# Causal mask by a GpSimd select on the exponentiated scores instead of mask matmuls, and both sets of dispatch writes in one block

## The chip, the cores and the metric

The program runs on one core of one Trainium2 chip. The metric is the device time of one execution in microseconds (us). A core has a matmul engine (TensorE, PE in the profile), a vector engine (VectorE, DVE), an activation engine (ScalarE, ACT), a general engine (GpSimd, POOL) and a queue that starts transfers (SyncE, SP). Each runs its own list of instructions in order and waits for the others on semaphores.

## The reference, cut to what matters

Two transformer-like layers on x (4, 1024, 128). Layer 0 is a state-space scan and a mixture of 16 experts. Layer 1 is attention with 16 heads of 8 with a bias by distance, then a block with causal attention and a top-2 mixture of 16 experts with capacity. The change touches two places of this last block:

```
scores = jnp.einsum('bhqd,bhkd->bhqk', q, k)
causal = jnp.tril(jnp.ones((s, s), bool))          # s = 1024 here
scores = jnp.where(causal, scores, neg)
attn = jax.nn.softmax(scores, axis=-1)
ctx = jnp.einsum('bhqk,bhkd->bhqd', attn, v)
hidden = resid + (ctx @ o_w + o_b)
...
xt = layer_norm(hidden, ln2_w, ln2_b).reshape(T, D)
...
xin = jnp.einsum('tec,td->ecd', dispatch, xt)      # each token to its two experts' slots
...
moe_out = jnp.einsum('tec,ecd->td', combine, eout)
return resid + moe_out
x = x + gb * that
```

## The kernel before

**Attention.** `attend` serves both attention layers; `a.causal` tells them apart. It works in 16 units, one for each batch b and group g of four heads. A unit has two passes that run in different units at the same time:

- Row maxima of a later unit: `top_turn` multiplies queries by keys for 128 queries and up to 512 keys, for two heads at once (L1095), and VectorE takes the maximum over the keys (L1199). When all turns of a unit are read, the maxima are transposed (L1088), negated (L1196) and moved by four transfers from SyncE (L1033) into the last row of the query operand, so that the second pass subtracts them inside its matmul.
- Scores, exponentials and values of this unit: `score_pair` multiplies keys by queries (L1123), so that the scores lie with 128 keys on the partitions and up to 512 queries along the row. ScalarE exponentiates them (L1236) from one of three PSUM banks into a ring of 16 slots in SBUF. `value_turn` multiplies the values by the exponentials and adds up in bank 7 (L1144).

A piece is one key tile i and one half of the queries; in the causal case queries before i * 128 are left out. The causal list has 12 pieces n: (i=0..3, first half), then (i=0..3, second half, all 512 wide), then (i=4..7, second half). Pieces 0 to 3 and 8 to 11 begin on the diagonal and are 512, 384, 256 and 128 wide; pieces 4 to 7 don't touch it. Each piece has four heads, so two calls of `score_pair` and four exponentials.

TensorE's order is written out in `run`: for each piece n and each pair of heads one `score_pair`, then the top turns that `plan_tops` puts there, then half of the value turn of piece n - LAG (LAG = 2; the last two pieces of a unit are valued in the first two pieces of the next). So the value turn of piece n comes behind the first score turn of piece n + 2. A score turn waits until the exponentials of the banks that it needs are done; a value turn waits for the four exponentials of its piece; exponentials wait for the value turn of four pieces ago, which frees their ring slots.

The causal mask is made on TensorE. `add_mask` adds four small bf16 matmuls behind a score or a top matmul on the diagonal: identity times a triangle of -1e30, in two halves of 64 rows, for two heads (L1105). GpSimd has one job in the causal stage, the copy of the next unit's values (L1250, `next_values`). In the biased layer it also multiplies exponentials by the bias near the diagonal (L1275, in `bias`), and there the value turn waits for it as well, on the semaphore `scaled`.

**Routing and experts.** `route` computes the two experts and slots of each token. GpSimd then writes the tokens into the experts' rows in DRAM, 32 indirect transfers for each of the two choices (`send_copies`, L1669). The first 32 are issued at the end of `route`. The block then ends, which is a barrier over all engines, and `experts` begins with the second 32, while VectorE multiplies the residual stream by its gate and adds it to x (L1850, L1852). SyncE waits there for all 64 and reads the first two experts' rows back (L1727).

**Constants.** One transfer loads all constants (`cst`), the mask parts among them; VectorE converts them to bf16 (`half`, L159).

Of the kernel before, what the change touches and what calls it, by code (L numbers as in the profile page):

```python
# [20 lines left out]
P = 128  # L21
# [3 lines left out]
TB = L // P  # L25
# [24 lines left out]
C_HALF = C_FLIP + P  # L50
C_W = C_HALF + 6 * P

# [801 lines left out]
def attend(nc, k, a):  # L854
# [44 lines left out]
    def near(n):  # L899

        i, half, q0, q1 = PIECES[n]
        lo, hi = max(q0, (i - 1) * P), min(q1, (i + 2) * P)
        return (lo, hi) if lo < hi and not causal else None
# [50 lines left out]

    NEARS = [n for n in range(NP_) if near(n)]

    with ExitStack() as c:
# [17 lines left out]
        stored = sem("stored")  # L975
        few_in, few_out, inverted = (sem(n) for n in ("few_in", "few_out", "inverted"))
        (a_filled, a_read, joined, b_filled, exped, scaled, pv_done, o_copied,
# [46 lines left out]
        with nc.Block() as block:  # L1024
# [48 lines left out]
            def _(pe):  # L1073
                first.tensor(pe)

                def top_turn(b, g, n):


                    turn = unit(b, g) * NA_ + n
                    slot = A_BANK + 2 * ((g * NA_ + n) % 2)  # L1080
                    if n == 0:
                        pe.wait_ge(loads[g], (b + 1) * NLOAD)

                    if not (isinstance(turn, int) and turn < 2):
                        pe.wait_ge(a_read, turn - 1)
                    if n == NT_:
                        pe.wait_ge(joined, unit(b, g) + 1)
                        nc.tensor.transpose(k.ps[0:HG * TB, slot, 0:P], top[:, 0, :, :].rearrange("p j i -> p (j i)"),  # L1088
                                            k.cst[:, C_ID:C_ID + P]).then_inc(a_filled, 1)
                        return  # L1090
                    pair, i, k0, k1 = TURNS[n]
                    diag = causal and k0 <= i * P < k1
                    for x in range(2):
                        rows = slice(64 * x, 64 * x + ROWS)
                        ins = nc.tensor.matmul(k.ps[:, slot + x, 0:k1 - k0], qop[rows, g, pair, i * P:(i + 1) * P],  # L1095
                                               kop[rows, g, pair, k0:k1], start=True, stop=not diag)
                    if diag:
                        ins = add_mask(slot, i * P - k0, 1)
                    ins.then_inc(a_filled, 1)

                def add_mask(bank, at, which):
                    for part in range(2):
                        for x in range(2):
                            rows = slice(64 * x, 64 * x + 64)
                            ins = nc.tensor.matmul(k.ps[:, bank[x] if isinstance(bank, tuple) else bank + x, at:at + P],  # L1105
                                                   k.half[rows, part, 0, :], k.half[rows, part, which, :],
                                                   start=False, stop=part == 1)
                    return ins

                def score_pair(b, g, n, pair):  # L1110
# [8 lines left out]
                    bank = (B_BANK + bank_of(g, t), B_BANK + bank_of(g, t + 1))  # L1119
                    diag = causal and q0 == i * P  # L1120
                    for x in range(2):
                        rows = slice(64 * x, 64 * x + ROWS + 1)
                        ins = nc.tensor.matmul(k.ps[:, bank[x], 0:q1 - q0], kop[rows, g, pair, i * P:(i + 1) * P],  # L1123
                                               qop[rows, g, pair, q0:q1], start=True, stop=not diag)
                    if diag:
                        ins = add_mask(bank, 0, 2)
                    ins.then_inc(b_filled, 1)
# [115 lines left out]
            def _(pool):  # L1243
# [20 lines left out]
                def bias(b, g):  # L1264

                    u = unit(b, g)
                    for n in NEARS:
                        i, half, q0, q1 = PIECES[n]
                        if n == NEARS[len(NEARS) // 2]:
                            next_values(b, g)  # L1270
                        lo, hi = near(n)
                        for j in range(HG):
# [7 lines left out]
                values(0, 0)  # L1280
                units(pool, next_values if causal else bias)

# [205 lines left out]
def route(nc, k, m, r):  # L1488
# [6 lines left out]
    with ExitStack() as c:  # L1495
        def sb(name, shape, dt=F32):
# [19 lines left out]
            ("logits", "e_ready", "chain", "ch_ready", "counts", "turned", "moved"))  # L1516
        ex_go, to_ready, ids_set = (nc.alloc_semaphore("ro_" + n) for n in ("ex_go", "to_ready", "ids_set"))

# [9 lines left out]
        with nc.Block() as block:  # L1528
# [32 lines left out]
            def _(act):  # L1561
# [16 lines left out]
                for b in range(B):  # L1578
                    ts = slice(b * TB, (b + 1) * TB)
                    nc.scalar.copy(r.xt[:, 1, ts, 0:D], r.xt[:, 0, ts, 0:D])  # L1580

            @block.gpsimd
            def _(pool):
# [6 lines left out]
                pool.wait_ge(act_plain, NT // 2)  # L1590
                send_copies(nc, k, r, 0)

            @block.vector
            def _(dve):
# [67 lines left out]
                L_(vec.tensor_scalar(col2[:], col2[:], KEEP, None, ALU.mult))  # L1662
                vec.tensor_tensor(r.g[:], r.g[:], col2[:].unsqueeze(1).broadcast_to([P, 2, NT]), ALU.mult)


# [15 lines left out]
def experts(nc, k, m, r):  # L1681
# [3 lines left out]
    with ExitStack() as c:  # L1685
        def sb(name, shape, dt=F32):
# [16 lines left out]
        got = [nc.alloc_semaphore(f"ex_got{s}") for s in range(4)]  # L1703
        first, both, gated, summed, x_plain, ids_kept, x_stored = (
            nc.alloc_semaphore("ex_" + n) for n in ("first", "both", "gated", "summed", "x_plain", "ids_kept", "x_stored"))
        chain = nc.alloc_semaphore("ex_chain")

        with nc.Block() as block:  # L1708
            @block.gpsimd
            def _(pool):  # L1710
                send_copies(nc, k, r, 1)
                for e in range(E):
# [132 lines left out]
            def _(dve):  # L1845

                for b in range(B):
                    h = r.hidden[:, b * TB:(b + 1) * TB, :]
                    xs = k.x[:, b * TB:(b + 1) * TB, :]
                    nc.vector.tensor_tensor(h, h, k.row[:, 2, b:b + 1, :].broadcast_to([P, TB, D]), ALU.mult).then_inc(chain, 1)  # L1850
                    dve.wait_ge(chain, b + 1)
                    nc.vector.tensor_tensor(xs, xs, h, ALU.add).then_inc(x_plain, 1)  # L1852
                dve.wait_ge(consts_in, 32)
# [24 lines left out]
                def add(n):  # L1878

                    xs = k.x[:, 4 * n:4 * n + 4, :]  # L1880
                    dve.wait_ge(gated, n + 1)
                    dve.wait_ge(x_plain, B)
                    nc.vector.tensor_tensor(xs, xs, back[:, 1, n % 4, :, :], ALU.add).then_inc(summed, 1)  # L1883
# [22 lines left out]
def causal_sublayer(nc, k, m):  # L1906
# [5 lines left out]
    with ExitStack() as c:  # L1912
# [28 lines left out]
        r.to = sb("to", [P, 2, NT], I32)  # L1941
        r.sent = nc.alloc_semaphore("cs_sent")
        r.g = sb("g", [P, 2, NT])
# [25 lines left out]
def program(nc, m):  # L1969
    with ExitStack() as c:  # L1970
# [15 lines left out]
        k.kop = sb("kop", [P, NG, 2, L], BF16)  # L1986
        k.half = sb("half", [P, 2, 3, P], BF16)

# [22 lines left out]
def constants():  # L2011
# [9 lines left out]
    a[:, C_MB:C_MB + P] = np.where(i[None, :] < i[:, None], NEG, 0.0)  # L2021
    half = a[:, C_HALF:C_W].reshape(P, 2, 3, P)
    for part in range(2):
        for base in range(2):
            rows = slice(64 * part, 64 * part + 64)
            for x, at in enumerate((C_ID, C_MA, C_MB)):
                half[64 * base:64 * base + 64, part, x] = a[rows, at:at + P]
# [81 lines left out]
```

## Time and profile before

| | us |
|---|---|
| median of 3 runs | 2185.87 (2176.83 to 2188.6) |
| the profiled execution's own time | 2184.34 |
| its span in the profile | 2182.5 |
| PE matmul busy over the span | 1741.0 |
| DVE busy | 1553.3 |
| ACT busy | 1188.9 |
| POOL busy | 765.8 |

Busy times are sums over stages with different limits. The causal attention stage lies from about 1355 to 1848 us of the span, the biased one ends near 1290, routing lies between 1884 and 2013, the experts after it. A row of the timeline gives start, duration of the merged instructions, engine, line, output and inputs, how many were merged, and in square brackets the idle time before them and who ended it. Rows of TensorE may overlap, since matmuls are pipelined; PEld is its weight load.

### The profile page before, as it was taken

The page shows a single profiled execution, that of the slowest core. Times are in us where ns is not written, and L with a number is a line of the kernel's source. Part 1 is how long each engine was busy: PE and PEld are TensorE (multiplying, and loading weights), DVE is VectorE, ACT ScalarE, POOL GpSimd, SP SyncE. Part 2 cuts the span into 40 slices and gives each one's busy share as a digit, 9 for nine tenths or more (in the row PEclk, how much of TensorE's full clock was granted, in tenths as well). Part 3 has the DMA queues.
Part 4 walks back from the last instruction along what each step waited for, and adds up shares of the span by engine and source line. Part 5 has one row for each costly group of instructions (what it writes and reads, how often), then busy time and mean ns, then how long its engine had stood idle before and what let it go on. Part 6 is the DMA issues. An engine that isn't in the chain of part 4 may idle for free. (4 is left out here: it accounts for less than half of the span.)

```text
span 2182.5 us, 45999 instructions
## 1 busy us (share of the span) xinstructions
PE 1741.0 (80%) x15779; PEld 799.5 (37%) x15780; DVE 1553.3 (71%) x2677; ACT 1188.9 (54%) x2290; POOL 765.8 (35%) x938
## 2 busy tenths in 40 slices
PE   5799999986899989989999545988998997500992
PEld 2666666652122222222222222333333332500671
DVE  4778887879899889989996288776776772551223
ACT  3232222242688878878888442776776776300432
POOL 1100000023577777767777432000000000156454
PEclk8799999997799999999999866999999999555996
DMA  2193000004010011001000305011111110411444
GB/s 78 59 136 78 0 0 0 0 21 129 16 36 19 19 24 31 19 20 36 19 19 14 88 22 144 19 37 24 32 37 37 36 23 15 125 35 52 128 133 135
DMA packets 93751, 103.52 MB, mean 47 GB/s; under 512 B 27137, under 2 KB 61649, under 8 KB 93041
## 3 DMA queue, kind: packets, MB, share of 16 engines
q1 hardware_dynamic: 89456, 92.46, 17.7%
q0 software_dynamic: 4096, 8.43, 1.1%
q8 instruction: 124, 2.03, 0.4%
q14 instruction: 75, 0.61, 0.1%
HBM read 63.78 MB, written 36.80 MB: 46 GB/s over the span
## 5 line engine op out<-in xcount | busy, mean ns | idle before, releaser
L1199 DVE TENSOR_REDUCE ba_at_top<-ps 128x2 f32<-128x1024 f32 x512 | 592.9, 1220 | 36.0 <-PE ps L1095 30.7
L1236 ACT ACTIVATE ba_at_ring<-ps 128x512 f32<-128x512 f32 x1024 | 556.5, 597 | 99.4 <-PE ps L1123 88.1
L1275 POOL TENSOR_TENSOR ba_at_ring<-ba_at_ring,rb_near 128x256 f32<-128x256 f32 (+2 forms) x640 | 480.2, 784 | 199.8 <-ACT ba_at_ring L1236 199.4
L1199 DVE TENSOR_REDUCE ca_at_top<-ps 128x2 f32<-128x1024 f32 (+3 forms) x384 | 355.2, 956 | 86.3 <-PE ps L1095 40.9
L1236 ACT ACTIVATE ca_at_ring<-ps 128x512 f32<-128x512 f32 (+3 forms) x768 | 335.9, 491 | 142.1 <-PE ps L1105 114.8
L1095 PE MATMUL ps<-kop,qop 48*128 48x512 bf16 (+3 forms) x1792 | 340.9, 381 | 71.5 <-DVE ba_at_top L1199 31.8
L1123 PE MATMUL ps<-qop,kop 49*128 49x512 bf16 (+3 forms) x1792 | 340.3, 376 | 60.5 <-ACT ca_at_ring L1236 14.5
L1144 PE MATMUL ps<-ba_at_ring,ba_at_low 128*32 128x256 f32 (+2 forms) x4096 | 340.6, 406 | 17.7 <-ACT ba_at_osb L1221 15.0
L1123 PEld LDWEIGHTS ps<-qop,kop 49*128 49x128 bf16 x1792 | 86.5, 93 | 433.5 <-ACT ba_at_ring L1236 247.7
L520 ACT ACTIVATE gm_sg<-ps,gm_bias 128x512 f32<-128x512 f32 x128 | 87.9, 687 | 235.1 <-PE ps L460 235.1
L1144 PE MATMUL ps<-ca_at_ring,ca_at_low 128*32 128x256 f32 (+1 forms) x2816 | 201.6, 359 | 5.2 <-ACT ca_at_osb L1221 4.3
L1250 POOL COPY ca_at_low<-ca_v 128x288 f32 (+1 forms) x16 | 7.2, 455 | 454.8 <-PE ps L1144 454.7
L604 DVE SCALAR_TENSOR_TENSOR gm_y<-ps,gm_w,gm_y 128x128 f32 (+1 forms) x512 | 144.0, 344 | 31.0 <-DVE gm_bef L377 16.8
L1144 PEld LDWEIGHTS ps<-ba_at_ring,ba_at_low 128*32 128x32 f32 x4096 | 82.7, 110 | 212.6 <-issue 145.7
L466 PEld LDWEIGHTS ps<-gm_w,gm_hc 128*128 128x128 f32 x1024 | 135.0, 192 | 62.6 <-issue 48.4
L1105 PE MATMUL ps<-half 64*128 64x128 bf16 x2048 | 144.9, 223 | 0.0
L1095 PEld LDWEIGHTS ps<-kop,qop 48*128 48x128 bf16 x1792 | 89.8, 95 | 145.8 <-DVE ba_at_top L1199 58.4
L466 PE MATMUL ps<-gm_w,gm_hc 128*128 128x128 f32 x1024 | 135.8, 276 | 0.7 <-DVE gm_hc L592 0.7
L459 PE MATMUL ps<-hT,gm_w 128*128 (+1 forms) x256 | 133.0, 602 | 0.0
L652 POOL TENSOR_TENSOR gm_gated<-gm_y,row 128x512 f32 x8 | 10.1, 1265 | 350.1 <-DVE gm_y L604 350.1
L460 PE MATMUL ps<-hT,gm_w 128*128 (+1 forms) x256 | 132.5, 599 | 0.0
L592 DVE SCALAR_TENSOR_TENSOR gm_hc<-ps,gm_bias,gm_sg 128x512 f32<-128x512 f32 x128 | 95.6, 747 | 43.3 <-ACT gm_sg L520 42.6
(317 smaller groups left out, 1749.2 us busy)
## 6 DMA issues: line engine op xcount, KB each, us to landing
cs_fc<-in_fc_w SPq DMA_DIRECT2D x32, 256.0 KB, 2.7
qk_parts<-ba_at_ring SPq DMA_DIRECT2D x24, 256.0 KB, 3.2
qop<-qk_parts SPq DMA_DIRECT2D x64, 96.0 KB
kop<-qk_parts SPq DMA_DIRECT2D x64, 96.0 KB
qk_parts<-ca_at_ring SPq DMA_DIRECT2D x24, 256.0 KB, 3.3
ex_xi<-expert_rows_in SPq DMA_DIRECT2D x16, 258.0 KB, 3.2
expert_rows_in<-gm_zero SPq DMA_DIRECT2D x1, 4096.0 KB
expert_rows_out<-gm_zero SPq DMA_DIRECT2D x1, 4096.0 KB
```

Source lines behind the costliest of these rows:

```text
L459: nc.tensor.matmul(k.ps[:, A + e % 2, :], w1[:, e, :], k.hT[:, tok], start=True, stop=True)
L460: nc.tensor.matmul(k.ps[:, C + e % 2, :], w3[:, e, :], k.hT[:, tok], start=True, stop=True).then_inc(up, 1)
L466: ins = nc.tensor.matmul(k.ps[:, O + e % 2, j * P:(j + 1) * P], hc[:, e % 2, j * P:(j + 1) * P], w2[:, e, :], start=True, stop=True)
L592: nc.vector.scalar_tensor_tensor(hc[:, e % 2, :], k.ps[:, C + e % 2, :], bias[:, 1, e:e + 1], sg[:, e % 2, :], ALU.add, ALU.mult).then_inc ...
L604: ins = nc.vector.scalar_tensor_tensor(yt, k.ps[:, O + e % 2, j * P:(j + 1) * P], w[:, t, e], yt, ALU.mult, ALU.add)
L1095: ins = nc.tensor.matmul(k.ps[:, slot + x, 0:k1 - k0], qop[rows, g, pair, i * P:(i + 1) * P], kop[rows, g, pair, k0:k1], start=True, stop= ...
L1105: ins = nc.tensor.matmul(k.ps[:, bank[x] if isinstance(bank, tuple) else bank + x, at:at + P], k.half[rows, part, 0, :], k.half[rows, part ...
L1123: ins = nc.tensor.matmul(k.ps[:, bank[x], 0:q1 - q0], kop[rows, g, pair, i * P:(i + 1) * P], qop[rows, g, pair, q0:q1], start=True, stop=n ...
L1144: ins = nc.tensor.matmul(k.ps[32 * j:32 * j + 32, O_BANK, s0 - half * CH:s1 - half * CH], vs[:, g % 2, var, i, j, :], ring[:, (n % (RING / ...
L1199: nc.vector.tensor_reduce(top[:, k0 // CH, 2 * pair:2 * pair + 2, i], k.ps[:, slot:slot + 2, 0:k1 - k0], AX.X, ALU.max).then_inc(a_read, 1)
L1236: nc.scalar.activation(ring[:, t % RING, 0:q1 - q0], k.ps[:, B_BANK + bank_of(g, t), 0:q1 - q0], ACT.Exp).then_inc(exped, 1)
L1275: ins = nc.gpsimd.tensor_tensor(w, w, a.near[:, g * HG + j, lo - (i - 1) * P:hi - (i - 1) * P], ALU.mult)
```

## The change

The score mask moves behind the exponential: for each diagonal piece GpSimd zeroes, in the ring, the entries with query before key in the first 128 columns of its four heads, in one select on the index. It waits for the fourth exponential of the piece, and the value turn of a diagonal piece waits for it on `scaled`. The copy of the next unit's values moves into the same loop, ahead of piece 8. The masks of the top turns stay matmuls. The second set of dispatch writes, and VectorE's gating of the residual, move from `experts` into the block of `route`. The triangle for the scores leaves the constants.

```diff
-C_W = C_HALF + 6 * P
+C_W = C_HALF + 4 * P
...
-    NEARS = [n for n in range(NP_) if near(n)]
+    NEARS = [n for n in range(NP_) if (PIECES[n][2] == PIECES[n][0] * P if causal else near(n))]
...
-                    diag = causal and q0 == i * P
                     for x in range(2):
                         rows = slice(64 * x, 64 * x + ROWS + 1)
                         ins = nc.tensor.matmul(k.ps[:, bank[x], 0:q1 - q0], kop[rows, g, pair, i * P:(i + 1) * P],
-                                               qop[rows, g, pair, q0:q1], start=True, stop=not diag)
-                    if diag:
-                        ins = add_mask(bank, 0, 2)
+                                               qop[rows, g, pair, q0:q1], start=True, stop=True)
...
                         if n == NEARS[len(NEARS) // 2]:
                             next_values(b, g)
+                        if causal:
+                            pool.wait_ge(exped, u * NB_ + (n + 1) * HG)
+                            pool.sem_inc(piece_in, 1)
+                            s = n * HG % RING
+                            w = ring[:, s:s + HG, 0:P]
+                            nc.gpsimd.affine_select(w, w, [[0, HG], [1, P]], ALU.is_ge, 0.0, base=0,
+                                                    channel_multiplier=-1).then_inc(scaled, 1)
+                            continue
...
-                units(pool, next_values if causal else bias)
+                units(pool, bias)
...
                 send_copies(nc, k, r, 0)
+                pool.wait_ge(to_ready, 2)
+                pool.wait_ge(copied, B)
+                send_copies(nc, k, r, 1)
...
+                dve.wait_ge(act_plain, NT // 2)
+                for b in range(B):
+                    h = r.hidden[:, b * TB:(b + 1) * TB, :]
+                    xs = k.x[:, b * TB:(b + 1) * TB, :]
+                    vec.tensor_tensor(h, h, k.row[:, 2, b:b + 1, :].broadcast_to([P, TB, D]), ALU.mult).then_inc(gated_h, 1)
+                    dve.wait_ge(gated_h, b + 1)
+                    vec.tensor_tensor(xs, xs, h, ALU.add).then_inc(r.x_plain, 1)
...
             @block.gpsimd
             def _(pool):
-                send_copies(nc, k, r, 1)
                 for e in range(E):
...
-    half = a[:, C_HALF:C_W].reshape(P, 2, 3, P)
+    half = a[:, C_HALF:C_W].reshape(P, 2, 2, P)
```

The value turn itself is unchanged: its line `if n in NEARS: pe.wait_ge(scaled, ...)` now also holds in the causal case, since `NEARS` is [0, 1, 2, 3, 8, 9, 10, 11] there and was empty.

## Rows read from the trace of the kernel before

**Rows 1.** Stretches, causal and biased attention: busy us and instructions, granted clock, DMA share.

```profile
1355.00:1848.00 493.00, 434.25 (x6245) 180.40 (x6243) 342.75 (x391) 346.75 (x796) 6.38 (x14) 0.96 0.13 30
640.00:1290.00 650.00, 549.59 (x5407) 155.09 (x5406) 532.99 (x558) 506.63 (x948) 455.42 (x608) 0.92 0.11 28
```

**Rows 2.** The page's groups: busy us, mean ns, idle before, releaser.

```profile
L1199 DVE TENSOR_REDUCE ba_at_top<-ps 128x2 f32<-128x1024 f32 x512 | 592.9, 1220 | 36.0 <-PE ps L1095 30.7
...
L1105 PE MATMUL ps<-half 64*128 64x128 bf16 x2048 | 144.9, 223 | 0.0
```

**Rows 3.** Waits in the causal stage: total us, times, longest.

```profile
PEld ps L1123 <- ACT ca_at_ring L1236: 147.0, 331, 2.2
ACT ca_at_ring L1236 <- PE ps L1105: 114.3, 203, 5.1
```

**Rows 4.** Timeline, second diagonal burst of a unit, pieces 8 to 10.

```profile
1722.38 0.28 PE L1105 MATMUL ps<-half 64*128 64x128 bf16 x4
1722.59 0.64 PE L1144 MATMUL ps<-ca_at_ring,ca_at_low 128*32 128x256 f32 x8
1723.16 0.39 PE L1123 MATMUL ps<-qop,kop 49*128 49x512 bf16 x2
...
1723.71 1.08 ACT L1236 ACTIVATE ca_at_ring<-ps 128x512 f32<-128x512 f32 x2 [0.32 <-PE ps L1105]
...
1724.38 0.34 PE L1123 MATMUL ps<-qop,kop 49*128 49x384 bf16 x2
...
1726.87 0.64 PE L1144 MATMUL ps<-ca_at_ring,ca_at_low 128*32 128x256 f32 x8
```

**Rows 5.** Timeline, end of the unit before: piece 8 and the transpose of the row maxima.

```profile
1693.73 1.09 ACT L1236 ACTIVATE ca_at_ring<-ps 128x512 f32<-128x512 f32 x2 [0.32 <-PE ps L1105]
...
1697.86 0.28 PE L1088 MATMUL ps<-cst,ca_at_top 128*32 128x128 f32 x1
```

**Rows 6.** Timeline, first diagonal burst of the next unit, from piece 0.

```profile
1702.37 0.39 PE L1123 MATMUL ps<-qop,kop 49*128 49x512 bf16 x2 [0.49 <-DMA qop<-ca_at_negm]
...
1703.00 3.29 ACT L1236 ACTIVATE ca_at_ring<-ps 128x512 f32<-128x512 f32 x6 [1.42 <-PE ps L1105]
...
1703.65 0.39 PE L1123 MATMUL ps<-qop,kop 49*128 49x512 bf16 x2 [0.20 <-ACT ca_at_ring L1236]
...
1705.51 0.43 PE L1144 MATMUL ps<-ca_at_ring,ca_at_low 128*32 128x128 f32 x8
...
1707.94 0.64 PE L1144 MATMUL ps<-ca_at_ring,ca_at_low 128*32 128x256 f32 x8 [0.31 <-ACT ca_at_osb L1221]
...
1714.32 0.43 PE L1144 MATMUL ps<-ca_at_ring,ca_at_low 128*32 128x128 f32 x8
```

**Rows 7.** Groups on GpSimd, shapes apart: busy us, mean ns.

```profile
L652 POOL TENSOR_TENSOR gm_gated<-gm_y,row 128x512 f32 x8 | 10.1, 1265 | 350.1 <-DVE gm_y L604 350.1
...
L230 POOL TENSOR_SCALAR n4xn<-cs_h,n4mean,n4rstd 128x128 f32<-128x128 f32 x8 | 6.7, 849 | 13.0 <-DVE n4shift L187 13.0
...
L1250 POOL COPY ca_at_low<-ca_v 128x288 f32 x12 | 5.5, 455 | 396.2 <-PE ps L1144 396.2
```

**Rows 8.** Who waited for the 640 multiplications of L1275 (us, times).

```profile
  PEld ps L1144: 21.4, 45
```

**Rows 9.** Groups in the causal stage, shapes apart.

```profile
L1199 DVE TENSOR_REDUCE ca_at_top<-ps 128x2 f32<-128x1024 f32 x180 | 219.0, 1224 | 70.4 <-PE ps L1095 40.9 <-PE ps L1105 25.9
```

**Rows 10.** Timeline, between the two sets of indirect writes.

```profile
1966.19 0.96 POOL L1669 DMA_INDIRECT expert_rows_in<-cs_xt,cs_to  x1 [0.30 <-issue]
...
1970.75 1.42 POOL L1669 DMA_INDIRECT expert_rows_in<-cs_xt,cs_to  x1 [3.60 <-POOLq L1528]
```

**Rows 11.** Timeline, last indirect write and first read-back.

```profile
2011.35 0.96 POOL L1669 DMA_INDIRECT expert_rows_in<-cs_xt,cs_to  x1 [0.30 <-issue]
2013.64 5.75 SPq L1727 DMA_DIRECT2D ex_xi<-expert_rows_in  x3
```

**Rows 12.** Transfers: KB each, us to landing.

```profile
cst<-in_consts SPq DMA_DIRECT2D x1, 976.0 KB, 5.3
```

More of the change, by code:

```diff
@@ L975, in attend @@
         stored = sem("stored")
-        few_in, few_out, inverted = (sem(n) for n in ("few_in", "few_out", "inverted"))
+        few_in, few_out, inverted, piece_in = (sem(n) for n in ("few_in", "few_out", "inverted", "piece_in"))
         (a_filled, a_read, joined, b_filled, exped, scaled, pv_done, o_copied,
@@ L1097, in top_turn, with add_mask @@
                     if diag:
-                        ins = add_mask(slot, i * P - k0, 1)
+                        ins = add_mask(slot, i * P - k0)
                     ins.then_inc(a_filled, 1)
-                def add_mask(bank, at, which):
+                def add_mask(slot, at):
                     for part in range(2):
@@ L1104, in add_mask @@
                             rows = slice(64 * x, 64 * x + 64)
-                            ins = nc.tensor.matmul(k.ps[:, bank[x] if isinstance(bank, tuple) else bank + x, at:at + P],
-                                                   k.half[rows, part, 0, :], k.half[rows, part, which, :],
+                            ins = nc.tensor.matmul(k.ps[:, slot + x, at:at + P], k.half[rows, part, 0, :], k.half[rows, part, 1, :],
                                                    start=False, stop=part == 1)
@@ L1516, in route @@
             ("logits", "e_ready", "chain", "ch_ready", "counts", "turned", "moved"))
-        ex_go, to_ready, ids_set = (nc.alloc_semaphore("ro_" + n) for n in ("ex_go", "to_ready", "ids_set"))
+        ex_go, to_ready, ids_set, copied, gated_h = (
+            nc.alloc_semaphore("ro_" + n) for n in ("ex_go", "to_ready", "ids_set", "copied", "gated_h"))
         def v(t):
@@ L1579, in _ @@
                     ts = slice(b * TB, (b + 1) * TB)
-                    nc.scalar.copy(r.xt[:, 1, ts, 0:D], r.xt[:, 0, ts, 0:D])
+                    nc.scalar.copy(r.xt[:, 1, ts, 0:D], r.xt[:, 0, ts, 0:D]).then_inc(copied, 1)
             @block.gpsimd
@@ L1703, in experts @@
         got = [nc.alloc_semaphore(f"ex_got{s}") for s in range(4)]
-        first, both, gated, summed, x_plain, ids_kept, x_stored = (
-            nc.alloc_semaphore("ex_" + n) for n in ("first", "both", "gated", "summed", "x_plain", "ids_kept", "x_stored"))
-        chain = nc.alloc_semaphore("ex_chain")
+        first, both, gated, summed, ids_kept, x_stored = (
+            nc.alloc_semaphore("ex_" + n) for n in ("first", "both", "gated", "summed", "ids_kept", "x_stored"))
         with nc.Block() as block:
@@ L1845, in _ @@
             def _(dve):
[L1847 to L1852, printed above, removed]
                 dve.wait_ge(consts_in, 32)
@@ L1881, in add @@
                     dve.wait_ge(gated, n + 1)
-                    dve.wait_ge(x_plain, B)
+                    dve.wait_ge(r.x_plain, B)
                     nc.vector.tensor_tensor(xs, xs, back[:, 1, n % 4, :, :], ALU.add).then_inc(summed, 1)
@@ L1941, in causal_sublayer @@
         r.to = sb("to", [P, 2, NT], I32)
-        r.sent = nc.alloc_semaphore("cs_sent")
+        r.sent, r.x_plain = nc.alloc_semaphore("cs_sent"), nc.alloc_semaphore("cs_x_plain")
         r.g = sb("g", [P, 2, NT])
@@ L1986, in program @@
         k.kop = sb("kop", [P, NG, 2, L], BF16)
-        k.half = sb("half", [P, 2, 3, P], BF16)
+        k.half = sb("half", [P, 2, 2, P], BF16)
         k.row_of = [(0, GA), (1, GA), (1, GB), (1, CB), (1, SB), (0, GB)]
@@ L2025, in constants @@
             rows = slice(64 * part, 64 * part + 64)
-            for x, at in enumerate((C_ID, C_MA, C_MB)):
+            for x, at in enumerate((C_ID, C_MA)):
                 half[64 * base:64 * base + 64, part, x] = a[rows, at:at + P]
```

## Prediction

> **What bounds the kernel now.** I read the page first, for the stages, then the stretch table of the two attention stages, then groups, waits and timeline inside the causal one, and last the chain for the routing. The causal stage lasts 493 us. In it TensorE has matmuls in flight 434 us, VectorE is busy 343 us, ScalarE 347 us and GpSimd 6 us, and the granted clock is 0.96, so nearly all of it is at 2.4 GHz [rows 1]. TensorE's queue is the bound, but not by much: the other two fill 70% each. The reader should see in the groups that mask matmuls are 2048 short instructions, half for the row maxima, which stay, and half for the scores, which go; one VectorE reduction of 1024 columns takes 1.22 us [rows 2]. The waits say who hands over to whom: ScalarE waits 114.3 us for the mask matmuls, TensorE's weight loads wait 147.0 us for the exponentials [rows 3]. This is a loop of score, mask, exponential and freed bank, so a mask that goes is taken either from TensorE's queue or from the latency in front of the exponentials; both shorten the turn.
>
> **Part one: the masks.** A unit (batch, head group) has 12 pieces in two bursts of four diagonal pieces (n = 0 to 3 and 8 to 11) with four full ones between. A diagonal piece has two turns with four mask matmuls each, so 16 sets per unit and 256 in all. What a set costs the queue is not its 0.28 us in flight but the distance to the next instruction: one starts at 1722.38, the value matmuls behind it at 1722.59, 0.21 us [rows 4]. 16 x 0.21 = 3.4 us per unit, 54 us in all: the ceiling.
>
> What comes back, per unit:
> - The next unit's first score waits for the row maxima by DMA. From the transpose at 1697.86 over VectorE's negation and SyncE's four DMAs to that score at 1702.37 are 4.5 us [rows 5, 6], fixed, and TensorE already idles 0.49 us at its end. The two sets of piece 11 lie inside it and shorten nothing: 0.42 us lost.
> - Pieces 0 and 8 are 512 wide. Six exponentials take 3.29 us, 0.55 each [rows 6], so a turn of two can't go under 1.10 us. The turns now take 1.28 (1702.37 to 1703.65) and 1.22 (1723.16 to 1724.38) [rows 4, 6]; 1.22 can fall by 0.12, not 0.21. Two of the four such turns are that near: about 0.2 us lost.
> - Top turns lie between score turns and each needs a bank that VectorE has read. In the full pieces nothing is removed; in the bursts I allow 0.2 us for a reduction that is now awaited.
> - Left: 3.4 - 0.42 - 0.2 - 0.2 = 2.6 us per unit, 41 us in 16 units.
>
> **The select.** GpSimd does one per diagonal piece, 8 per unit, 128 in all, on 128 x (4 x 128) f32 in place, behind the fourth exponential of the piece; the value turns of that piece now wait for it. The trace has no select. The nearest rows are: a copy of 288 columns in 0.455 us, which as a rate is 0.81 for 512; a two-input multiply of 512, 1.27 us; and a tensor-scalar op of 128 columns that takes 0.85, which as a rate would be 3.4 us for 512 [rows 7]. A select reads one input, computes an index and writes: I take 1.1 us, between copy and two-input multiply, and keep 0.45 (the copy as it stands, for fewer columns) and 3.4 as ends.
>
> Does 1.1 us fit? LAG puts the value turn of piece n behind the first score turn of n+2. Piece 0: its four exponentials start at 1703.00 and end at 1705.2, its value turn is at 1707.94 [rows 6]: 2.7 us, some 2.1 with the masks gone. Piece 8: exponentials end at 1724.8 (1723.71 + 1.08), value turn at 1726.87 [rows 4]: 2.07 us, some 1.6 afterwards. The others have more. So a select up to about 1.45 us, with 0.1 for semaphores, is hidden; piece 8 is the tight one. Behind the waiting select on GpSimd is only the next unit's value copy (0.455 us, now placed ahead of piece 8, needed a third of a unit later). Behind the waiting value turn is everything else on TensorE. In the biased stage, which has the same wait with GpSimd at 455 of 650 us [rows 1], TensorE's weight loads waited 21.4 us for it over 160 pieces (640 multiplications in fours) [rows 8], 0.13 us a piece; at GpSimd's much lower load here (8 x 1.1 of 27 us) I charge 4 us in all and keep 17 us (0.13 x 128) as the bad end. VectorE's reduction is not slowed by a busy GpSimd: 1220 ns in the biased stage, 1224 here [rows 2, 9].
>
> The Trainium skill (GPSIMD Engine Reference, section 7, Performance pitfalls for Q7 kernels) gives a compare-and-select body 2.03 cycles per element, 1.03 unrolled; as an estimate 512 x 2.03 / 1.2 GHz is 0.87 us, and by it the sum is the same, since all of it would be hidden. No row here shows such a body.
>
> **Part two: routing.** Before, the first 32 indirect writes end at 1967.15 and the next starts at 1970.75, behind the block's barrier; two writes in one block are 0.30 apart, so 3.3 us go. The second set of rows is ready and the copy done long before. The eight gating operations go from VectorE's start of the next block to its end of this one; they ran beside the writes before and do so now. But the barrier now comes after the last write. Before, SyncE was already in the block and read back 1.3 us after the last issue (2011.35 + 0.96 to 2013.64) [rows 10, 11]; now it must pass the barrier, some 3 us by GpSimd's own 3.3. That gives 1.7 back: 1.6 us gained; the ends are 0 and 3.3.
>
> **Part three: constants.** They lose 256 of 1952 columns, 0.13 of 0.98 MB of a transfer that lands in 5.3 us [rows 12], and a later one ends the wait there: 0.4 us, between 0 and 0.7. The smaller conversion on VectorE is hidden or worth 0.1.
>
> **Sum.** 41 - 4 + 1.6 + 0.4 = 39 us. The profiled execution took 2184.34 us (a span of 2182.5 and 1.8 around it), 1.5 below the median of 2185.87. 2184.34 - 39 = 2145; against the median 2147. I predict 2146.
>
> **Rivals.**
> 1. Slow select; this is the other side. The mechanism is GpSimd's queue: four selects back to back are done 4(S + 0.1) after piece 0's exponentials, and the value turn of piece 3 was at 1714.32, 9.1 us after 1705.2 [rows 6]. At S = 3.4, 14.0 - 9.1 = 4.9 us late. The second burst has 10.7 us, from 1694.8 (1693.73 + 1.09) to piece 11's value turn at 1705.51 [rows 5, 6]: 3.3 late. 8.2 x 16 = 131 us longer, less 2 for the rest: 2313. It decides from S = 2.2, where 4(S + 0.1) passes 9.1. For it speaks the tensor-scalar row, against it the copy and the multiply. The Trainium skill (GPSIMD Engine Reference, section 3.1) says that data-dependent branching costs about 12 cycles per element, by estimate 5.1 us for 512: this rival and worse; an index comparison need not branch, and no row shows it. Chance 0.16.
> 2. Select of some 1.8 to 2.3 us: piece 8 stalls 0.4 to 0.9 us per unit and the first burst gives its saving back; 2175 to 2197. Chance 0.08.
> 3. The saving is met by VectorE, or the wait comes as in the biased stage. If only the second burst shortens (8 x 0.21 - 0.42 = 1.3 us per unit), 20 us, and with part two 2162; with 17 us of waits for selects 41 - 17 + 2 gives 2158. For it: VectorE at 70% on average and higher between the bursts; against it: its idle time at the transpose. Chance 0.16.
> 4. The forecast, chance 0.60. Its own range: 54 + 4 gained is 2126, 27 gained is 2157.
>
> **Range.** Rivals 2 and 3 reach up to 2178; down, the ceiling with both other parts whole gives 2126, and the scatter of the three runs before (2176.83 to 2188.6) takes off 4 more: 2122. Rival 1 is left out. About 0.5%, 11 us, is what a measurement here can tell from no change. Faster 0.76, same 0.08, slower 0.16.
>
> **What would show it.** In the profile after: 1024 mask matmuls; a stage of about 455 us instead of 493; a select near 1.1 us; TensorE's wait for GpSimd under 5 us in total, most at piece 8; the wait for the row maxima up by 0.4 us per unit; the gap of 3.6 us between indirect writes gone and one of about 1.6 more ahead of the first read-back. Wrong makes it a select above 1.5 us, first of all, then a VectorE that has no slack in the bursts.

## The result, and the profile after

The changed kernel takes 2163.82 us (median of 7 runs, 2159.19 to 2182.26) against 2184.14 us of the kernel before in the same comparison (7 runs). The ratio of the runs is 0.993, 95% interval 0.9909 to 0.9951: it is faster by 0.5 to 0.9%. The medians lie 20 us apart, the ratio says 15; the forecast was 39. The time is inside the range of the prediction, but that is no merit of its sum: the range was wide, and the gain is 0.4 to 0.5 of what was forecast. The execution that was profiled is the slowest of the seven (2182.26, span 2180.5), so a second profile of the same kernel (e1, span 2156.7) is used beside it.

The whole causal stage of the profiled execution, then of e1 (same columns as [rows 1]; they answer to its first row, 493 us with 434.25 us of matmuls at a clock of 0.96):

```profile
1355.00:1843.00 488.00, 428.46 (x5204) 157.21 (x5200) 338.19 (x389) 345.77 (x792) 85.45 (x140) 0.89 0.12 30
```

```profile
1347.00:1819.00 472.00, 411.05 (x5197) 154.00 (x5193) 336.66 (x387) 345.29 (x792) 85.70 (x140) 0.94 0.13 31
```

A thousand matmuls are gone and the stage is 5 us shorter in one execution and 21 us in the other. What differs most between the two is the clock, 0.89 against 0.94. The groups of the profiled execution, where [rows 2] had 2048 mask matmuls:

```profile
L1105 PE MATMUL ps<-half 64*128 64x128 bf16 x1024 | 78.0, 234 | 0.0
...
L1272 POOL TENSOR_SCALAR_AFFINE_SELECT ca_at_ring<-ca_at_ring 128x512 f32<-128x512 f32 x128 | 81.3, 635 | 426.7 <-ACT ca_at_ring L1232 426.7
```

The select takes 0.635 us. Who waited for it (us, times), which answers to [rows 8]:

```profile
who waited for it (us, times):
  PE ps L1140: 0.4, 1
  PEld ps L1140: 0.4, 2
```

The tight case of the prediction was piece 8. Its select and its value turn in the timeline after, in the unit that ends at 1446:

```profile
1439.23 0.64 POOL L1272 TENSOR_SCALAR_AFFINE_SELECT ca_at_ring<-ca_at_ring 128x512 f32<-128x512 f32 x1 [12.44 <-ACT ca_at_ring L1232]
...
1440.81 0.64 PE L1140 MATMUL ps<-ca_at_ring,ca_at_low 128*32 128x256 f32 x8
```

The select ends 0.94 us ahead of the value turn. So it is hidden, and most of the loss is elsewhere. Waits in the stage, against [rows 3]:

```profile
PEld ps L1121 <- ACT ca_at_ring L1232: 155.2, 327, 2.5
ACT ca_at_ring L1232 <- PE ps L1121: 131.6, 186, 4.6
...
PE ps L1121 <- DMA qop<-ca_at_negm: 15.7, 15, 3.5
```

ScalarE used to wait for the masks and now waits for the scores themselves, in all for about as long. The kernel before had a second row, in which it waited for scores, and the two make 135.1 us against 131.6 now:

```profile
ACT ca_at_ring L1236 <- PE ps L1123: 20.8, 49, 0.5
```

**A unit at full clock.** The distance between two sends of the row maxima (SyncE, L1033) is the period of a unit. Timeline of the profiled execution:

```profile
1413.59 2.69 SPq L1033 DMA_DIRECT2D qop<-ca_at_negm  x4
...
1442.28 2.67 SPq L1033 DMA_DIRECT2D qop<-ca_at_negm  x4
```

28.69 us, and the same in e1; before it was 29.94 to 29.98 in most units. That is 1.27 us less per unit, where 2.6 were forecast. Turn by turn, from one first score matmul to the next (us), in the unit that starts at 1702.37 before and the one that starts at 1417.46 after:

| turn | before | after | | turn | before | after |
|---|---|---|---|---|---|---|
| piece 0 | 1.28, 1.20 | 1.16, 1.09 | | piece 8 | 1.48, 1.22 | 1.48, 1.11 |
| piece 1 | 1.11, 1.04 | 1.00, 0.92 | | piece 9 | 1.13, 1.03 | 1.01, 0.93 |
| piece 2 | 1.51, 0.90 | 1.60, 0.79 | | piece 10 | 0.96, 2.42 | 0.84, 2.30 |
| piece 3 | 0.96, 0.85 | 0.86, 0.73 | | piece 11 | 0.79, 1.64 | 0.68, 1.72 |

Thirteen turns lose 0.10 to 0.12 us each, never 0.21. The other three lose nothing, and two of them are longer by 0.08 and 0.09. The first turn of piece 2 holds the first value turn into bank 7, which waits for ScalarE's copy out of it. The first of piece 8 waits for VectorE. The second of piece 11 ends with the wait for the row maxima. Here is the first and the third in the timeline after (the idle in the brackets of the value turn was 0.31 in [rows 6], that of the score 0.49):

```profile
1422.66 0.64 PE L1140 MATMUL ps<-ca_at_ring,ca_at_low 128*32 128x256 f32 x8 [0.52 <-ACT ca_at_osb L1217]
...
1446.14 0.39 PE L1121 MATMUL ps<-qop,kop 49*128 49x512 bf16 x2 [0.66 <-DMA qop<-ca_at_negm]
```

**Unit borders.** The 14 intervals are counted from the second send of the stage. Behind every fourth unit the hardware loop turns round, and TensorE has a gap in which, for the most part, it waits for nothing that the profile shows ("issue"):

```profile
1505.72 0.61 PE L1121 MATMUL ps<-qop,kop 49*128 49x512 bf16 x2 [2.83 <-issue]
```

The fifth and ninth interval hold it: 34.68 and 35.12 us before, 39.17 and 38.47 in the profiled execution, 34.16 and 34.57 in e1. The eleventh was 30.0 before, 35.76 in the profiled execution and 33.20 in e1; there the transfer of the row maxima was late. All 14 make 429.3 us before, 428.4 in the profiled execution and 416.9 in e1: the profiled execution lost nearly all that its units had gained. The clock around the first of these borders, in steps of 5 us (last but two column), before:

```profile
1510.00:1515.00 5.00, 1.67 (x34) 0.70 (x29) 1.94 (x3) 0.89 (x4) 0.00 (x0) 0.82 0.04 8
1515.00:1520.00 5.00, 4.36 (x44) 1.95 (x46) 2.18 (x2) 2.17 (x4) 0.00 (x0) 0.50 0.01 3
1520.00:1525.00 5.00, 4.32 (x76) 2.02 (x72) 2.96 (x4) 3.89 (x11) 0.46 (x1) 1.00 0.13 23
```

and after:

```profile
1500.00:1505.00 5.00, 2.80 (x42) 1.09 (x40) 3.05 (x4) 0.89 (x4) 1.25 (x2) 0.95 0.04 10
1505.00:1510.00 5.00, 4.28 (x40) 1.59 (x44) 2.19 (x2) 2.61 (x6) 0.64 (x1) 0.50 0.02 5
...
1520.00:1525.00 5.00, 4.68 (x44) 1.69 (x42) 3.06 (x4) 3.94 (x8) 0.00 (x0) 0.50 0.16 40
1525.00:1530.00 5.00, 4.85 (x38) 1.53 (x42) 2.91 (x5) 2.54 (x6) 0.00 (x0) 0.50 0.02 3
1530.00:1535.00 5.00, 4.81 (x50) 1.49 (x51) 3.97 (x5) 3.02 (x7) 0.00 (x0) 0.82 0.01 2
```

The granted clock falls from 2.4 to 1.2 GHz in the gap in both. Before it was back after 6.8 us; in the profiled execution after it stayed low for 27.3 us, with matmuls in flight nearly all the time. Over all kernels of this document (the experiments are below), read in steps of 0.5 us, the clock was at 1.2 GHz behind the two loop borders for (us):

| kernels in which TensorE's units are in the loop | first | second |
|---|---|---|
| score masks: before, e3, e4, e5, e10 | 6.8, 6.8, 6.8, 3.4, 6.8 | 6.8, 3.4, 3.4, 3.4, 3.4 |
| masks in every fourth unit, the one behind the border: e11 | 10.2 | 10.2 |
| no score masks: after, e1, e2, e6 | 27.3, 10.2, 13.7, 13.7 | 23.9, 10.2, 10.2, 13.7 |

**Routing.** Timeline of the profiled execution, last indirect write and first read-back, against [rows 11]:

```profile
2007.79 0.96 POOL L1684 DMA_INDIRECT expert_rows_in<-cs_xt,cs_to  x1 [0.30 <-issue]
2014.27 0.93 SPq L1740 DMA_DIRECT2D ex_xi<-expert_rows_in  x2
```

The gap of 3.60 us in [rows 10] is gone, and 5.5 us lie now between the end of the last write and the read-back, where there were 1.3. From the first indirect write to the first transposition of the experts it was 92.1 us (1924.65 to 2016.76) and is 92.8 (1924.35 to 2017.17). By this pair the second part lost 0.7 us.

### The profile page after: what moved, and what is told of

Its sections match the earlier page's. It is cut to its first block and busy times, and to the rows that moved or that the text cites. A ratio compares the mean times of both kernels' runs of the same rounds, so it can differ in the third digit from the quotient of the medians.

```text
span 2180.5 us, 44433 instructions
## 1 busy us (share of the span) xinstructions
PE 1738.9 (80%) x14756; PEld 779.7 (36%) x14756; DVE 1550.2 (71%) x2677; ACT 1189.3 (55%) x2290; POOL 846.4 (39%) x1066
## 5 line engine op out<-in xcount | busy, mean ns | idle before, releaser
L1095 PE MATMUL ps<-kop,qop 48*128 48x512 bf16 (+3 forms) x1792 | 348.6, 390 | 70.8 <-DVE ba_at_top L1195 31.4
L1121 PE MATMUL ps<-qop,kop 49*128 49x512 bf16 (+3 forms) x1792 | 346.6, 383 | 60.9 <-DMA qop<-ca_at_negm 15.7
L1272 POOL TENSOR_SCALAR_AFFINE_SELECT ca_at_ring<-ca_at_ring 128x512 f32<-128x512 f32 x128 | 81.3, 635 | 426.7 <-ACT ca_at_ring L1232 426.7
L1140 PE MATMUL ps<-ca_at_ring,ca_at_low 128*32 128x256 f32 (+1 forms) x2816 | 214.4, 380 | 7.4 <-ACT ca_at_osb L1217 6.2
L466 PEld LDWEIGHTS ps<-gm_w,gm_hc 128*128 128x128 f32 x1024 | 135.1, 193 | 62.5 <-issue 48.4
L1728 POOL DMA_INDIRECT expert_rows_out<-ex_eo,ex_to x64 | 61.3, 957 | 77.1 <-DVE ex_eo L1877 62.2
```

The costliest lines, as they stand in the source:

```text
L466: ins = nc.tensor.matmul(k.ps[:, O + e % 2, j * P:(j + 1) * P], hc[:, e % 2, j * P:(j + 1) * P], w2[:, e, :], start=True, stop=True)
L1140: ins = nc.tensor.matmul(k.ps[32 * j:32 * j + 32, O_BANK, s0 - half * CH:s1 - half * CH], vs[:, g % 2, var, i, j, :], ring[:, (n % (RING / ...
```

## The experiments

The theories were these. A: a mask set costs the queue 0.11 us instead of 0.21, and the clock at the borders does the rest. B: VectorE or ScalarE takes the saving back. C: the barrier behind the last indirect write costs more than the gap between the sets. All ratios are to the kernel before, with their 95% intervals.

**e1, the changed kernel again.** No edit.

> The changed kernel once more, to have a profile of an execution near its median. Theory A (a mask set costs the queue 0.11 us, not 0.21, and TensorE's clock stays at 1.2 GHz for a whole unit at some unit borders): units at full clock last 28.7 us again, the time follows the number of half-clock units at about 4 to 5 us each, so an execution near 2164 us has one or two fewer of them than the three of the 2182 us execution. Theory B (VectorE or ScalarE takes the saving back everywhere): the full-clock units themselves differ between a 2182 and a 2164 us execution.

2162.69 us (ratio 0.9901, 0.9874 to 0.9928). The units at full clock are 28.7 us as in the first profile; the sum of the 14 intervals is 416.9 us against 428.4, and the whole difference of 11.5 is in the fifth, ninth and eleventh interval as told above. A is right that within the stage the execution to execution difference is at the borders; it is not the number of half-clock units that differs but how long each lasts. B, in the form that the units themselves would differ, is out. The stages ahead of this one, in which no instruction has changed, also scatter: the first exponential of the causal stage was at 1360.9 us before, at 1358.5 in the profiled execution and at 1348.8 here. Of the 23.8 us between the spans of the two executions of the changed kernel, 9.7 lie ahead of the stage and 11.5 in it.

**e2, part one alone.** The writes and the gating stay where they were:

```diff
             def _(pool):
+                send_copies(nc, k, r, 1)
                 for e in range(E):
```

> Part one and the smaller constants alone; the dispatch writes stay in two blocks. If part two is worth the 1.6 us of the prediction, this is 1.6 us slower than both together. Theory C (the barrier behind the last write costs more than the 3.3 us that go between the sets: read-back 5.5 us after the last issue instead of 1.3): this is 0.9 us faster than both together, about 17 to 21 us below the kernel before.

2167.09 us (0.9936, 0.9909 to 0.9963). Periods of 28.7 us, borders 35.18 and 34.32. From the first indirect write to the experts' first transposition: 92.2 us. It is 16 us below the kernel before by the medians and 14 by the ratio, where 17 to 21 were expected. Theory C had this 0.9 us faster than both parts together; the medians have it 3 to 4 us slower, but its ten executions spread over 24 us (2157.41 to 2181.78), so the times say nothing about part two.

**e3, part two alone**, on the kernel before:

```diff
                 send_copies(nc, k, r, 0)
+                pool.wait_ge(to_ready, 2)
+                pool.wait_ge(copied, B)
+                send_copies(nc, k, r, 1)
```

> Part two alone on the kernel before. Theory C: 0.5 to 1 us slower than before, the first transposition of the experts some 0.7 us later counted from the first indirect write. The prediction's step: 1.6 us faster. Both are below what the times can tell; the trace decides.

2181.53 us (0.9984, 0.9966 to 1.0001): as expected, nothing that the times can tell. The trace decides: 93.0 us from the first write (1923.27) to the first transposition, against 92.1 before and 92.2 in e2. Timeline:

```profile
2006.86 0.96 POOL L1680 DMA_INDIRECT expert_rows_in<-cs_xt,cs_to  x1 [0.30 <-issue]
2013.34 0.93 SPq L1736 DMA_DIRECT2D ex_xi<-expert_rows_in  x2
...
2016.26 1.11 PE L1785 MATMUL ps<-cst,ex_xi 128*128 128x128 f32 x4 [86.72 <-DMA ex_xi<-expert_rows_in]
```

The same 5.5 us. C holds in the traces: 0.6 to 0.9 us are lost, not 1.6 gained.

**e4, select and masks**: the kernel before with the select added and the score masks kept.

> The kernel before with the select added and the score masks kept. If the select of 0.64 us is wholly hidden: unit period 29.96 us and the time of before within 0.2%, clock dips as short as before. If the select's wait costs what the biased stage's does (0.13 us a piece): 17 us slower, period 31.0 us. Theory A has the difference between this and the changed kernel, 1.27 us a unit, as 16 sets at 0.11 less what is lost.

2183.28 us (0.9988, 0.9968 to 1.0008). The period is 30.03 to 30.08 us, 0.1 more than before. Who waited for the select (us, times):

```profile
  PE ps L1144: 0.4, 1
```

The select costs 0.1 us a unit, under 2 us in all. It is paid at one place, the first value turn of piece 2. That turn is 1.60 us here and in the changed kernel and 1.51 before, because the value turn starts 0.23 us after the end of ScalarE's copy (1424.30 + 0.59) instead of 0.14. Timeline of e4:

```profile
1424.30 0.59 ACT L1221 COPY ca_at_osb<-ps 128x512 f32<-128x512 f32 x1
...
1425.12 0.64 PE L1144 MATMUL ps<-ca_at_ring,ca_at_low 128*32 128x256 f32 x8 [0.41 <-ACT ca_at_osb L1221]
```

What remains for the masks is 30.07 - 28.69 = 1.38 us a unit, 0.086 a set. The clock was back as soon as before (6.8 and 3.4 us at 1.2 GHz behind the two borders), as expected: the select does not keep it low. Over the whole span it was 0.890 on average in the ten executions of e4 and in the 25 of the kernel before, and 0.882 in the ten of e2, which has the select and no score masks.

**e5, every score mask set twice**, on the kernel before:

```diff
                     if diag:
+                        add_mask(bank, 0, 2, last=False)
                         ins = add_mask(bank, 0, 2)
```

> The kernel before with every score mask set issued twice (the triangle is added twice). The prediction's price, 0.21 us a set: the unit period goes from 29.96 to up to 33.3 us. Theory A, 0.11 us or less a set, since two 64-row matmuls run beside each other: 31.2 to 31.7 us. Theory B (the queue has slack, and the period is set by VectorE or ScalarE): nearly 29.96.

2205.04 us (1.0098, 1.0061 to 1.0134), 22 us slower. The period is 31.32 us, 1.36 more for 16 sets: 0.085 a set. The lengths in flight show the price of a set directly; timeline of e5, a double score set and a single one behind a top turn:

```profile
1420.98 0.39 PE L1105 MATMUL ps<-half 64*128 64x128 bf16 x8
...
1421.37 0.28 PE L1105 MATMUL ps<-half 64*128 64x128 bf16 x4
```

Four more matmuls, 0.11 us more. Turn by turn, the same thirteen turns are 0.10 to 0.12 us longer than before, and the same three are not. 0.21 is out, and so is a queue with slack.

**e6, part one with GAP 1.** The transpose of the row maxima (L1088) one turn behind the last top turn instead of three:

```diff
-    GAP = 3
+    GAP = 1 if causal else 3
```

> Part one alone, with the transpose of the row maxima one turn behind the last top turn instead of three (GAP 1 in the causal stage). VectorE waited 2.0 us for that transpose and TensorE 0.66 us for the transfer behind it. If the border wait is what is left of each unit: period 28.7 to about 28.0 us, stage 10 us shorter, and the 3.5 us waits at single borders, with their half-clock unit, gone. If TensorE only waits for the last reduction instead: no change.

2149.09 us (0.9835, 0.9803 to 0.9867), 18 us less than e2. The period is 27.76 us, 0.9 less, more than the 0.66 us of the wait. Turn by turn, 0.73 went at the border (the second turn of piece 11 is 0.99 instead of 1.72) and 0.19 where the transpose moved (the second turns of pieces 9 and 10 are 1.92 and 1.12 instead of 0.93 and 2.30). The late transfers are gone as well, the eleventh interval is 27.84. Waits of e6:

```profile
DVE ca_at_negm L1192 <- PE ps L1088: 6.2, 15, 0.6
...
PE ps L1121 <- DMA qop<-ca_at_negm: 0.7, 1, 0.7
```

The first of these was 29.9 us, the last 15.7. The loop borders stay, at 35.08 and 35.34 us. Now the select begins to show: TensorE and its weight loads waited 4.5 us for it in 12 places, against 0.8 in 3. Timeline of e6 at the first value turn behind a unit border, piece 10 of the unit before:

```profile
1437.08 0.16 PEld L1140 LDWEIGHTS ps<-ca_at_ring,ca_at_low 128*32 128x32 f32 x8 [0.43 <-POOL ca_at_ring L1272]
```

**e7, part one, TensorE's causal units written out without the hardware loop**:

```diff
-                units(pe, run)
+                units(pe, run, flat=causal)
```

> Part one alone, with TensorE's instructions of the causal stage written out without the hardware loop. Theory A: the issue gaps of 3 to 4 us every fourth unit and the half-clock units behind them go; all borders are near 28.7 us, and it is 12 to 20 us faster than part one with the loop. Rival: without the loop TensorE still has the gaps where it has to fetch instructions, at other places; no change.

2163.05 us (0.9908, 0.9878 to 0.9938), 4 us less than e2, where 12 to 20 were expected. The fifth interval is 29.18, the ninth 32.44; the others are 28.2 to 28.8, and 29.2 once. These are of its fastest execution (2152.67, mean clock 0.889). The other three took 2162 to 2167 us at 0.879 to 0.882, so there the clock was low for longer, with the loop gone; no trace shows where.

**e8, the same with the masks**, on the kernel before.

> The kernel before with TensorE's causal instructions written out in the same way. Theory A: periods near 29.96 us everywhere, some 10 to 14 us faster than before; the distance to part one without the loop is then 16 x 1.27 = 20 us, with no share of the clock in it. Rival: the clock gives more back with masks than without, then the distance stays at about 16 us.

2174.23 us (0.9948, 0.9924 to 0.9973). Borders 30.85 and 30.93, others 29.57 to 29.99, the last 30.80. Its whole stage, with a clock of 0.98:

```profile
1355.00:1839.00 484.00, 429.93 (x6281) 178.70 (x6275) 339.37 (x387) 348.62 (x801) 6.39 (x14) 0.98 0.13 30
```

The gap at the border is 1.0 us of the interval, where it was 5. The sum of the 14 intervals is 420.9 us against 404.3 in e7, 16.6 us or 1.2 per interval, but e7's is of its fastest execution. In the times the distance to e7 is 11 us by the medians and 9 by the ratios, less than the 20 of theory A and the 16 of the rival, though the intervals are too wide to tell it from 16. The mean clock is 0.892 in its eight executions and 0.883 in the four of e7: with the code written out, too, the kernel with masks has the higher clock. That speaks for the rival.

**e9, part one, written out, GAP 1.** Both edits.

> Part one with TensorE's causal instructions written out and GAP 1. If the two savings add: no wait for the row maxima, all periods near 27.7 us, stage some 13 us shorter than with either alone, 2138 to 2145 us. Rival: with the border wait gone the instruction fetch of the long code shows as new issue gaps, and it is no faster than GAP 1 alone (2149 us).

2144.38 us (0.9826, 0.9802 to 0.9849), the fastest here. The intervals are 27.3 to 27.8, the borders 29.14 and 29.25, the sum 390.0 us, 13 less than e6 and 14 less than e7. In the times it is 5 us below e6, and the intervals of the two ratios overlap. The trace, in which the two add, is again of the fastest execution (2134.98; the others 2142 to 2149), so that they add is shown for that one and not for the usual one.

**e10, the kernel before with GAP 1.** The one edit of e6.

> The kernel before, masks and all, with GAP 1 in the causal stage. If the wait at the unit border is one of before too, only smaller: period 29.96 to about 29.3 us, 8 to 12 us faster than before, and the distance to part one with GAP 1 grows from 16 to 20 to 25 us. If the border wait matters only once the masks are gone: no change.

2168.85 us (0.992, 0.9893 to 0.9946). The period is 29.12, 0.84 less. The wait at the unit border was there before, and the distance to e6 is 20 us by the medians, 19 by the ratios.

**e11, e6 with the score masks kept beside the select in the units with g = 1**, which follow a loop border:

```diff
-                    diag = causal and q0 == i * P
+                    diag = causal and q0 == i * P and g == 1
```

> Part one with GAP 1 and the loop, the score masks kept beside the select in the units with g = 1, which are those behind a loop border. Theory A (mask columns behind a gap bring TensorE's clock back sooner): the border interval exceeds the period by 4 to 5 us instead of 7.4; the masks cost 1.3 us in four units, so the total is 0 to 5 us less than 2149. Rival: the excess stays near 7 us and the total rises by 5.

2157.59 us (0.9885, 0.9864 to 0.9906), 8 us more than e6. The borders are 35.08 and 35.62, as long as without the masks. By the expectation that is the rival, but the comparison leaves out the masks' own time: they make the same interval 1.0 us longer where no loop border is in it (the first one is 28.62, in e6 27.60). And the clock did come back sooner. First e6, then e11:

```profile
1495.00:1500.00 5.00, 4.21 (x40) 1.53 (x41) 2.19 (x2) 2.55 (x5) 0.64 (x1) 0.50 0.02 5
1500.00:1505.00 5.00, 4.63 (x40) 1.32 (x38) 2.78 (x3) 3.07 (x9) 0.69 (x2) 0.50 0.15 26
1505.00:1510.00 5.00, 4.59 (x62) 1.83 (x60) 2.81 (x4) 2.73 (x8) 1.63 (x3) 0.75 0.47 122
```

```profile
1500.00:1505.00 5.00, 4.70 (x56) 2.13 (x56) 2.64 (x3) 3.04 (x6) 0.64 (x1) 0.63 0.01 3
1505.00:1510.00 5.00, 4.84 (x49) 1.83 (x47) 2.39 (x3) 2.59 (x7) 0.80 (x2) 0.50 0.19 33
1510.00:1515.00 5.00, 4.59 (x70) 2.02 (x72) 3.05 (x4) 2.97 (x8) 1.51 (x3) 0.85 0.51 124
```

It was at 1.2 GHz for 10.2 us at both borders, in e6 for 13.7. But 10.2 us was also seen in e1 and e2, without masks, and it is not the 3.4 to 6.8 us of the kernels that keep them all. So e11 neither shows nor refutes this half of theory A.

## Why the prediction was wrong

**The step that failed** is the first term of the sum, the price of a mask set, which was taken at about twice its size: "16 x 0.21 = 3.4 us per unit, 54 us in all: the ceiling". The distance of 0.21 us at 1722.38 was read at a mask set of a top turn in front of a value turn. It holds 0.11 us of masks and 0.10 us that TensorE spends on going from the 64-row matmuls to the value matmuls, and this is paid whatever stands in front of the value turn. Had the term been read at a score mask set in front of a top turn, in the same unit of the kernel before, it would have been 0.11:

```profile
1723.39 0.28 PE L1105 MATMUL ps<-half 64*128 64x128 bf16 x4
...
1723.50 0.38 PE L1095 MATMUL ps<-kop,qop 48*128 48x512 bf16 x2
```

That the 0.10 is paid by the value turn itself shows in the changed kernel, where 512 columns of a top turn stand in front of one: 0.31 us to the value turn, against 0.23 us from a score of 512 columns to the next matmul (1437.55 to 1437.78).

```profile
1437.78 0.38 PE L1095 MATMUL ps<-kop,qop 48*128 48x512 bf16 x2
...
1438.09 0.64 PE L1140 MATMUL ps<-ca_at_ring,ca_at_low 128*32 128x256 f32 x8
```

e5 measured the 0.11 directly and e4 and e5 the 0.085 to 0.086 us that a set is worth on average, since three turns of sixteen are set by something else. The four mask matmuls use two halves of 64 rows. Scores of 128, 256, 384 and 512 columns take 0.07, 0.12, 0.17 and 0.23 us to the next matmul, some 0.053 for each 128; as an estimate from that, four times 128 columns one after the other would be 0.21 us, and two and two side by side are 0.11. The Trainium skill (TensorEngine Tiling (Array Packing), Key Properties) says that different tiles can execute weight loads and matmuls in parallel; e5's row agrees, 0.39 us for eight against 0.28 for four. With 0.11 in the prediction's own sum, two sets lost at the border (0.22), 0.2 for VectorE and none for ScalarE, whose 1.10 us would not have bound, it would have been 1.76 - 0.42 = 1.34 us per unit, 21 us; 1.27 was measured. At full clock 16 units at 1.27 are 20 us, where 37 were forecast for part one; what the clock took beyond that is below.

**What came back.** The three deductions were 0.82 us together. Measured against 16 x 0.11 = 1.76 it is 0.49: 0.33 for three turns that lost nothing, and 0.17 by which two of them grew. The three are the border, VectorE at piece 8 as expected, and the copy out of bank 7 at piece 2, which the prediction didn't have; the 0.09 at piece 2 is the select's (e4). It had ScalarE's pace at pieces 0 and 8 instead, and that did not bind, since the turns came to 1.09 to 1.16 us.

**The select.** 1.1 us was taken, 0.635 measured, well above the low end (0.45), and it is hidden, as the step said; 4 us were charged for its wait and under 2 came (e4). Rivals 1 and 2 are out. The nearest row was the copy, not the multiply.

**Rival 3** named the right size, 20 us, for the wrong reason. VectorE sets one of the three turns that gave nothing; it did not halve the gain.

**The border** was seen as a fixed latency of 4.5 us, rightly; the wait grew from 0.49 to 0.66, not by 0.4, since a set is worth half. The prediction took it as a loss of 0.4 us and did not see that it was the larger prize: the transpose stood two turns of the queue further back than it had to, with VectorE idle for 2.0 us in each unit. e6 took 18 us there with one number.

**The clock** is the second failed step: the prediction had it at 2.4 GHz for nearly the whole stage and gave it no term, without a reason. It was 0.89 over the stage in the profiled execution and 0.94 in e1, against 0.96 before (the stage lasted 488 and 472 us, where 455 were forecast), and it took back a part of the gain. In size this is an estimate. e2 and e4 both have the select and differ in the score masks; by their mean clocks, 0.882 and 0.890, e2 was at 1.2 GHz for some 30 us more (2 x (1 - clock) x time, 510 us against 479). Between the profiled execution and e1 38 us more at 1.2 GHz, in the three intervals named above, went with 11.5 us more time, 0.3 us each. That makes some 9 us of the 22 (16 x 1.38) that the missing masks gave at full clock, and leaves 13; the times have 16 between e4 and e2 by the medians and 11 by the ratios.

That kernels without score masks stay low for longer holds at every traced border at which TensorE's loop turns round (10.2 to 27.3 us in eight, 3.4 to 6.8 in ten with masks), and these borders exceed the period by 5.4 to 10.5 us without masks and by 3.2 to 5.4 with them. Why is open: masks in the unit behind the border alone gave 10.2 us (e11), doubled masks 3.4 (e5). What decides the length from one execution to the next is open too.

**Part two** had the wrong sign: +1.6 us forecast, -0.6 to -0.9 measured in the traces (after, e2, e3). The failed step is the barrier, "some 3 us by GpSimd's own 3.3"; 5.5 us pass, counted from the end of the last write. What the 2.5 us more consist of the traces don't show, and it was not tried.

**Part three**, 0.4 us, is below the scatter of the earlier stages (10 us between the first exponentials of two executions of the changed kernel) and stays untested.

## What to carry to other kernels

The price of an instruction in a full queue is the distance to the next one at the very place where it goes, with the neighbour that it has there; what the next instruction pays for its own change of tile shape (0.10 us here) does not go when the one in front of it goes. Before taking work off an engine, look for the waits in which all engines stand still together (a transposed row by DMA at a unit border, a loop that turns round): here one constant was worth as much as a thousand matmuls. Compare the granted clock before and after as well: the kernels here with fewer matmuls had it low for longer. Two blocks merged into one did not remove the barrier here but moved it, from a gap of 3.6 us between writes to one of 5.5 us behind the last.

## What the runs showed of the hardware

A GpSimd select on the index of 128 x 512 f32 in place takes 0.635 us, less than a two-input multiply of the same size (1.265 us). A set of four mask matmuls of 128 columns in two halves of 64 rows takes 0.11 us of TensorE's queue, and a value turn of 128x32 tiles 0.10 us beyond the columns in front of it. With TensorE's units written out, about 1 us is left of the gap at the loop border, which was 5 us of the interval (e8). The granted clock fell to 1.2 GHz at the gaps of 2.7 to 3.9 us at the loop borders, in or just behind them, and stayed there for 3.4 to 6.8 us in kernels with the score masks and for 10.2 to 27.3 us in those without.
